# Perceiver block on one core: the last two pipeline steps written as one tail

## What is computed

```python
x = x + fake_quant(layernorm(x)) @ fake_quant(context)        # context: 1024 x 1024 per sequence
h = layernorm(x); qkv = h @ Wqkv                              # 32 query heads of 32, one k and one v head
x = x + softmax(q k^T * scale + alibi, causal) v @ Wo
h = layernorm(x)
routing = softmax(h @ gate_w.T)                               # 8 experts
x = x + (h * (routing @ in_scale)) @ sign(weight).T * (routing @ out_scale) + bias
```

## Time and profile before

| | us |
|---|---|
| median of 3 runs (range) | 446.04 (445.1 to 447.58) |
| the profiled execution | 443.82 |
| its span on the core | 442.0 |
| mean granted TensorE clock | 0.972 |
| PE busy / DVE / ACT / POOL | 372.8 / 308.6 / 258.2 / 96.0 |

### The profile page before, as it was taken

One profiled execution on the slowest core, in us unless ns is written; L12 is line 12 of the kernel. 1 busy time (PEld: TensorE's weight loads), 2 busy tenths in 40 slices (PEclk: granted clock), 3 DMA queues, 4 the chain that ended last, 5 costly groups with the idle time before them and its releaser, 6 DMA issues.

```text
span 442.0 us, 9600 instructions
## 1 busy us (share of the span) xinstructions
PE 372.8 (84%) x3952; PEld 255.0 (58%) x3952; DVE 308.6 (70%) x586; ACT 258.2 (58%) x308; POOL 96.0 (22%) x116
## 2 busy tenths in 40 slices
PE   0444957996999989998999999999999899889565
PEld 0114936953736946694659555965587558745332
DVE  7658579989856278786878688858785965394331
ACT  4777898747778655765666576757575722241010
POOL 5210010003403203140314041403231312031202
PEclk9999997999899999999999999999999999999859
DMA  7999998799399854675477547774681010001001
GB/s 313 385 381 409 408 380 325 258 364 340 139 366 347 297 177 164 249 239 184 159 285 231 190 149 255 267 216 144 213 313 27 0 49 2 3 1 49 0 0 47
DMA packets 30097, 91.97 MB, mean 208 GB/s; under 512 B 8224, under 2 KB 8224, under 8 KB 30048
## 3 DMA queue, kind: packets, MB, share of 16 engines
q1 hardware_dynamic: 27888, 83.40, 53.4%
q10 hardware_dynamic: 2160, 7.87, 4.7%
HBM read 85.50 MB, written 4.19 MB: 203 GB/s over the span
## 4 chain that ended last, share of the span: by engine, by line
PE 62%; DVE 16%; DMA 8%; ACT 5%; issue 5%; SPq 3%; POOL 0%; POOLq 0%; DVEq 0%; ACTq 0%
PE R L1512 10%; DMA ring<-ctx 7%; PE T L1335 7%; PE R L1286 7%; PE R L1287 6%; PE R L1288 6%; PE R L1374 5%; PE R L1377 5%; PE R L1376 5%; PE C L1316 4%; PE T L1468 4%; ACT b L524 3%; SPq L348 2%; DVE Pr L982 2%; DVE Wo L830 1%
## 5 line engine op out<-in xcount | busy, mean ns | idle before, releaser
L524 ACT ACTIVATE b<-ring,quant,qpar 128x2048 uint8<-128x2048 f32 x64 | 132.9, 2090 | 11.3 <-DMA ring<-ctx 8.5
L1374 PE MATMUL R<-T_hi,Wqkv_hi 128*128 128x128 f16 x448 | 78.8, 222 | 0.0
L1376 PE MATMUL R<-T_lo,Wqkv_hi 128*128 128x128 f16 x448 | 78.8, 222 | 0.0
L1377 PE MATMUL R<-T_hi,Wqkv_lo 128*128 128x128 f16 x448 | 78.7, 222 | 0.0
L1512 PE MATMUL R<-sgn,XS_hi 128*128 128x512 fp8e4 x128 | 49.7, 388 | 0.0
L1512 PE MATMUL R<-sgn,XS_lo 128*128 128x512 fp8e4 x128 | 49.5, 387 | 0.0
L1316 PE MATMUL C<-b,aT 128*64 128x512 f16 x256 | 37.8, 423 | 13.2 <-ACT b L524 11.2
L1374 PEld LDWEIGHTS R<-T_hi,Wqkv_hi 128*128 128x128 f16 x448 | 45.1, 101 | 0.4
L316 POOL TENSOR_TENSOR Pr<-Pr,mx 128x512 f32<-128x512 f32 x16 | 16.7, 1042 | 130.2 <-DVE mx L987 130.2
L1376 PEld LDWEIGHTS R<-T_lo,Wqkv_hi 128*128 128x128 f16 x448 | 44.5, 99 | 0.2
L1377 PEld LDWEIGHTS R<-T_hi,Wqkv_lo 128*128 128x128 f16 x448 | 44.5, 99 | 0.0
(11 more groups left out here) (145 smaller groups left out, 879.9 us busy)
## 6 DMA issues: line engine op xcount, KB each, us to landing
ring<-ctx SPq DMA_DIRECT2D x64, 1024.0 KB, 6.3
ring<-L_attn_Wo SPq DMA_DIRECT2D x4, 1024.0 KB, 7.7
ring<-L_ffn_weight SPq DMA_DIRECT2D x4, 1024.0 KB, 5.0
out<-X ACTq DMA_DIRECT2D x8, 512.0 KB, 2.6
Wo<-L_attn_Wqkv SPq DMA_DIRECT2D x7, 544.0 KB, 15.7
X<-x ACTq DMA_DIRECT2D x7, 512.0 KB, 4.0
sgn<-L_attn_Wqkv SPq DMA_DIRECT2D x1, 544.0 KB, 18.4
X<-x SPq DMA_DIRECT2D x1, 512.0 KB, 12.7
```

Of the source, the lines that this page charges most:

```text
L524: e.activation(b8[:, c % BRING, :], ring[:, slot, :], ACT.Identity, scale=qR2, bias=qZ2).then_inc(s_rf[slot], 1)
L1374: e.matmul(dst, hi, rows[0], start=k == 0 and g == 0, stop=False, skip_group_check=True)
L1376: e.matmul(dst, hi, rows[1], start=False, stop=False, skip_group_check=True)
L1377: last = e.matmul(dst, lo, rows[0], start=False, stop=k == KT - 1, skip_group_check=True)
```

## The change

- PE, ACT, DVE and POOL each get a function tail that replaces steps 8 and 9. Steps 0 to 7 are as before.
- Tile 6's sign burst writes C0 and C1 in place of R2 and R3, so pv no longer waits for tile 6's results. Its first half runs as 16 matmuls at the start, ahead of the outscale pair. Its second half is issued in pieces of k: 0-1 after the first pt, 2-3 after the last pv, 4-5 after the projections, 6 after t2, 7 after the router.
- The projections run first half low, ta 1, first half high, second half low, second half high.
- The second norm is written into tok in two halves, each with its own semaphore count; t2's second half waits for the second; the router's k 4 to 7 wait for the second copy.
- The scaled rows of tile 7 are made in three parts of 2, 2 and 4 k (the last one's scales in R3); the output scale pair of tile 7 is ahead of its burst.
- Tile 7's sign burst has three column groups: 512, 256 and 256 columns (R2, C0, C1). It runs k 0-1 of all groups first, then k 2-7 of each. Results follow in three parts; the last sum is on DVE, the other two on POOL.
- SP stores tile 6 (after both sums) and tile 7 in three stores, of 512, 256 and 256 columns. In the kernel before ACT issues one store for each tile.

```diff
@@ SP
-            e.wait_ge(s_out, 16 * TILES)
+            e.wait_ge(s_y, (TILES - 1) * 2)
+            store(TILES - 2, slice(0, H))
+            for n in range(2):
+                e.wait_ge(s_y, (TILES - 1) * 2 + n + 1)
+                store(TILES - 1, last_cols[n])
+            e.wait_ge(s_end, 1)
+            store(TILES - 1, last_cols[2])
+            e.wait_ge(s_out, 16 * (TILES + 2))
@@ POOL
+            def tail(t):
+                subtract_max(e, t, 0, 1)
+                subtract_max(e, t, 1, 1)
+                total(t - 1, 0)
+                inv_std(2, t)
+                with_bias(t)
+                total(t - 1, 1)
+                x_t = X[t % XBUFS]
+                for n in range(2):
+                    cols = last_cols[n]
+                    e.wait_ge(s_fe, t * 2 + n + 1)
+                    e.tensor_tensor(x_t[:, cols], x_t[:, cols], XL[:, cols], ALU.add).then_inc(s_y, 1)
@@ ACT
+                if t == TILES - 1:
+                    e.wait_ge(s_y, t * 2)
+            def tail(s, last):
+                exp(s, 0, 0)
+                outscale_copy(s)
+                pt_hi(s, 0, 0)
+                exp(s, 0, 1)
+                exp(s, 1, 0)
+                pt_hi(s, 0, 1)
+                exp(s, 1, 1)
+                pt_hi(s, 1, 0)
+                pt_hi(s, 1, 1)
+                ta_hi(s, 0)
+                ta_hi(s, 1)
+                t2_copy(s, 0)
+                t2_copy(s, 1)
+                router_exp(s)
+                rt_copy(s)
+                e.wait_ge(s_ffn, (TILES - 1) * 2)
+                for c, rows in enumerate(last_rows):
+                    e.wait_ge(s_xs, (TILES - 1) * 2 + c + 1)
+                    hi_part(XS[0][:, rows, :], ln2T[:, rows, :], 1.0, s_xshi)
+                outscale_copy(last)
@@ DVE
+            def tail(s):
+                t = TILES - 1
+                softmax_rest(t)
+                pt_lo(s, 0, 0)
+                result(s, 0)
+                pt_lo(s, 0, 1)
+                attn_rows(s, 0, 0)
+                pt_lo(s, 1, 0)
+                attn_rows(s, 0, 1)
+                pt_lo(s, 1, 1)
+                attn_rows(s, 1, 0)
+                ta_lo(s, 0)
+                attn_rows(s, 1, 1)
+                ta_lo(s, 1)
+                x2(s, 0)
+                x2(s, 1)
+                last_norm2(t)
+                router_max(s)
+                router_probs(s)
+                result(s, 1)
+                last_xs(0)
+                last_xs(1)
+                last_xs_lo(0)
+                last_xs(2)
+                last_xs_lo(1)
+                last_xs_lo(2)
+                for n in range(3):
+                    last_result(n)
+                x_t, cols = X[t % XBUFS], last_cols[2]
+                e.wait_ge(s_fe, t * 2 + 3)
+                e.wait_ge(s_x2b, TILES)
+                e.tensor_tensor(x_t[:, cols], x_t[:, cols], XL[:, cols], ALU.add).then_inc(s_end, 1)
@@ PE
-                if b == 1 and m > 1:
+                if b == 1 and 1 < m < TILES - 1:
                     e.wait_ge(s_fe, (m - 1) * 2 + h + 1)
...
+            def last_ffn(n, chunks):
+                cols = last_cols[n]
+                if n > 0 and chunks[0] == 0:
+                    e.wait_ge(s_fe, (TILES - 2) * 2 + n)
+                for c in chunks:
+                    e.wait_ge(s_xslo, c + 1)
+                    for k in range(last_rows[c].start, last_rows[c].stop):
+                        for part in range(2):
+                            last = e.matmul(last_sums[n], XS[part][:, k, :], sgn[:, k, cols],
+                                            start=k == 0 and part == 0, stop=k == KT - 1 and part == 1)
+                if k == KT - 1:
+                    last.then_inc(s_ffn, 1)
+
+            def tail(s, last):
+                ffn(s, 0, low)
+                ffn(s, 0, high)
+                outscale(s, 0)
+                outscale(s, 1)
+                pt(s, 0, 0)
+                ffn(s, 1, low[:2])
+                pt(s, 0, 1)
+                pv(s, 0, 0)
+                pt(s, 1, 0)
+                pv(s, 0, 1)
+                pt(s, 1, 1)
+                ta(s, 0)
+                pv(s, 1, 0)
+                pv(s, 1, 1)
+                ffn(s, 1, low[2:])
+                project(s, 0, low)
+                ta(s, 1)
+                project(s, 0, high)
+                project(s, 1, low)
+                project(s, 1, high)
+                ffn(s, 1, high[:2])
+                t2(s)
+                ffn(s, 1, high[2:3])
+                router(s)
+                ffn(s, 1, high[3:])
+                router_t(s)
+                for c in range(3):
+                    last_inscale(s, c)
+                outscale(last, 0)
+                outscale(last, 1)
+                for n in range(3):
+                    last_ffn(n, [0])
+                for n in range(3):
+                    last_ffn(n, [1, 2])
```

More of the change, by code:

```diff
@@ L285, in build @@
         s_y = sem("s_y")
+        s_xslo = sem("s_xslo")
+        s_end = sem("s_end")
         s_free = [sem(f"s_free{k}") for k in range(2)]
@@ L335, in query_to, with ffn_to, last_scales @@
             return C[:, n, :] if i == 1 else R[:, 2 + n, :]
+        def ffn_to(t, n):
+            return C[:, n, :] if t == TILES - 2 else R[:, 2 + n, :]
+        last_sums = (R[:, 2, :], C[:, 0, 0:HALF // 2], C[:, 1, 0:HALF // 2])
+        last_cols = (slice(0, HALF), slice(HALF, 3 * HALF // 2), slice(3 * HALF // 2, H))
+        last_rows = (slice(0, 2), slice(2, 4), slice(4, KT))
+        def last_scales(c):
+            return R[:, 3, :] if c == 2 else T[:, Step(TILES).bank(f"is{c}"), 0:HALF // 2]
         def queries_at(i, n):
@@ L395, in _, with store @@
             run_steps(first_half, lambda s: None)
-            e.wait_ge(s_out, 16 * TILES)
+            def store(t, cols):
+                e.dma_start(out_v[t, :, cols], X[t % XBUFS][:, cols]).then_inc(s_out, 16)
+            e.wait_ge(s_y, (TILES - 1) * 2)
[6 more added lines that the diff above has]
+            e.wait_ge(s_out, 16 * (TILES + 2))
         dq = 1.0 / (C_W * C_LN)
@@ L475, in first_half @@
                     return step_1()
-                if s.i < 3:
+                if s.is_step(TILES):
+                    return tail(TILES - 1)
+                if s.i < 3 or s.i > TILES:
                     return
@@ L743, in step_1 @@
                 conv(3, 1)
+            def tail(s, last):
[19 more added lines that the diff above has]
+                outscale_copy(last)
             def first_half(s):
                 f, m, b = s.front, s.middle, s.back
-                if s.i < 3:
+                if s.is_step(TILES):
+                    return tail(s, Step(TILES + 1))
+                if s.i < 3 or s.i > TILES:
                     return
@@ L765, in second_half @@
                     return step_1(s, Step(2))
+                if s.i >= TILES:
+                    return
                 f, m, b, n = s.front, s.middle, s.back, s.next
@@ L1031, in x2, with last_norm2 @@
                     stats(2, x_m, (1,))
+            def last_norm2(m):
+                e.wait_ge(s_Ta, TILES * 2)
+                e.wait_ge(s_rstd[2], m + 1)
+                for n in range(2):
+                    cols = slice(n * HALF, (n + 1) * HALF)
+                    e.tensor_scalar(tok[:, cols], X[m % XBUFS][:, cols], mv[2][:, 0:1],
+                                    rstd[2][:, 1:2], ALU.subtract, ALU.mult).then_inc(s_xl2, 1)
             def norm2(s):
                 m = s.i - 1
[L1035 to L1038, removed]
+                e.wait_ge(s_T1, s.i * 2 + 2)
                 if s.is_step(2):
@@ L1081, in result, with last_xs, last_xs_lo, last_result @@
                 e.wait_ge(s_ffn, t * 2 + n + 1)
-                e.scalar_tensor_tensor(XL[:, cols], R[:, 2 + n, :], 1.0 / C_XS, XL[:, cols],
+                e.scalar_tensor_tensor(XL[:, cols], ffn_to(t, n), 1.0 / C_XS, XL[:, cols],
+                                       ALU.mult, ALU.mult).then_inc(s_fe, 1)
+            def last_xs(c):
+                e.wait_ge(s_is, (TILES - 1) * 2 + c + 1)
+                rows = ln2T[:, last_rows[c], :].rearrange("p k t -> p (k t)")
+                e.scalar_tensor_tensor(rows, last_scales(c), C_XS, rows, ALU.mult, ALU.mult)                    .then_inc(s_xs, 1)
+            def last_xs_lo(c):
+                e.wait_ge(s_xshi, (TILES - 1) * 2 + c + 1)
+                rows = last_rows[c]
+                lo_part(XS[1][:, rows, :], ln2T[:, rows, :], XS[0][:, rows, :], 1.0, s_xslo)
+            def last_result(n):
+                cols = last_cols[n]
+                e.wait_ge(s_ose, TILES)
+                e.wait_ge(s_ffn, (TILES - 1) * 2 + n + 1)
+                e.scalar_tensor_tensor(XL[:, cols], last_sums[n], 1.0 / C_XS, XL[:, cols],
                                        ALU.mult, ALU.mult).then_inc(s_fe, 1)
@@ L1098, in softmax_rest @@
                 row_max(m, 1, 1)
+            def tail(s):
[30 more added lines that the diff above has]
```

(32 more changed lines are left out.)

5 lines of the change are left out of this document (3 added, 2 removed).

## The result

| | before | after |
|---|---|---|
| median (range, runs) | 446.81 (445.1 to 449.0, 4) | 441.4 (440.7 to 442.98, 4) |
| profiled execution, span | 443.82, 442.0 | 441.02, 439.2 |
| mean granted clock | 0.972 | 0.973 |

The ratio is 0.9896 with a 95% interval of [0.9864, 0.9928]. That is 4.6 us of 446.04, the median that stood in the profile before; a fourth run of the kernel before (449.0) has moved its median since, so the two medians of the table lie 5.4 us apart, which is inside the interval too. The forecast for the median was 442.9, from a difference of -3.1 us; the range held.

What follows compares the result with a forecast made beforehand. PE was taken to bound the kernel up to step 7, then full-clock matmuls to 412.4 us, then dependent operations. Terms +1.5 - 0.75 - 1.5 - 0.35 - 2.0 = -3.1 us, applied to the 446.04 median: 442.9 us, range 441.0 to 446.3.

Steps and rivals of the forecast that it cites:

- A: Tile 7's attention and projections, to the second residual sum: 1.5 us longer, from a 1.6 us PE stall behind ta 1.
- The attention front: Tile 7's attention ahead of the first projection: projections start as before, valued at 0, bounds -0.7 and +1.5 us.
- R2: Rival: exp, copy and transpose chain ahead of the projections grows by 1.5 us; 444.4 us, chance 18%.
- B: Second residual sum to the router's end: 0.75 us shorter, router starting about 4.8 us after the sum's start at 1.2 GHz.
- R1: Rival: PE's clock is kept through the second norm, router 1.90 us in place of 3.57; 441.2 us, chance 14%.
- C: Router's end to tile 7's first burst matmul: 1.5 us shorter (0.9 to 1.7), through smaller first scaled-row operations.
- D: Tile 7's sign burst: 0.35 us shorter, one outscale now being ahead of it; 1.3 us to either side.
- that bound: Tile 7's burst: 256-column matmuls take half of 0.217 us, at worst 0.1 more for some of 32, +1 us.
- E: Last matmul to the end of the span: 2.0 us shorter, 1.1 before the last store's issue and 0.9 in the store.
- R4: Rival: the short last stores save nothing (0.9 us less gain), 256-column matmuls cost 0.5 more; 444.3 us, chance 9%.
- R3: Rival: the clock falls in the attention stretch, projections doubled for 2.6 to 5.2 us; 448.0 us, chance 9%.

Runs made afterwards that it cites:

- b1_order: The kernel before with only first half high moved directly behind ta 1 and second half low after it: 447.74 us, ratio 1.0035.
- a1_order: The changed kernel with the projections in the order of before, second half low right behind ta 1: 439.13 us, ratio 0.9832 to the kernel before.
- a1_again: The same kernel as a1_order, measured once more: 439.95 us, ratio 0.9854 to the kernel before.
- a4_two_parts: The changed kernel with tile 7's scaled rows in two parts of 4 k in place of 2, 2 and 4: 443.18 us, ratio 0.9937.
- a2_one_store: The changed kernel with tile 7 written by one 512 KB store from SP after all three sums: 442.16 us, ratio 0.9923.
- b0_same: The kernel before, unchanged, measured again with a second profile: 446.37 us, ratio 0.9989.

## Why the prediction was right

*A, forecast +1.5.* Right in its parts. The wait behind ta 1 was 2.07 us from start to start for 2.05, and b1_order and a1_order show its price from both sides, +1.65 and -1.66. The attention front, which I valued at 0, gave -0.38: projections start 12.53 us after step 8's start, 12.91 before. R2 (the front longer by 1.5) did not happen. So 0 was the right order of size, and the 0.38 are inside my bounds.

*B, -0.75.* The sum is nearly right, its course was not, and that is luck. With the clock at 1.00 in the transposes and 0.50 in the router, as I assumed, a1_order shows 4.82 and 8.36, my 4.8 and -0.76. In the changed kernel the clock fell before the transposes (router start +5.99) and was back for the router (2.02): 1.2 us lost, 1.5 won. R1 thus came in half: not kept, but won back early. In a1_again it came whole, for the same idle 2.62 us, so its 14% was a chance between executions and not between kernels. Of the rows that I held against it, 62.5 to 66.0 and 107.0 to 110.5 show 0.99 and 0.97: the 0.50 comes only behind them. The two halves of the norm took 1.00 us together, 0.56 to the handover of the first.

*C, -1.5.* Measured -1.44; a4_two_parts gives 0.95 of it back, so about two thirds are the smaller first part. That the rest is the output scale that went ahead is reckoned and not tested: in before's trace it stands 0.54 us ahead of the burst's start (427.05 to 427.59).

*D, -0.35.* Measured -0.11. The time at 1.2 GHz behind the burst's start was 4.0 us in place of the 3.5 I took over from before; that is the difference. 256-column matmuls start 0.11 apart, half of 0.217, so that bound wasn't needed.

*E, -2.0.* Measured -2.01: 1.2 us from last matmul to store, as counted, and 2.2 from there. R4 (no gain from short stores) falls with a2_one_store. The Trainium skill, "DMA: Bandwidth & Descriptors", under "Anatomy of one DMA", has 2.0 us plus the bytes, and gives this for transfers issued from GpSimd, which I should have said; these stores are issued by SP. Here a 128 KB store landed in 1.8, a 512 KB one in 2.6. The measurement decides: 2.3 is too long for them, and the 1.6 to 1.7 behind my -0.9 was 0.1 to 0.2 too short.

*R3* (the clock lost in the attention stretch) was seen in none of the traces of the changed kernel or its variants; the one fall in step 8 was in the kernel before, b0_same, where it cost 1.26 us. My 2.6 to 5.2 count 12 or 24 projections at half speed; the 3.53 us of the earlier trace rows that I took them from hold eight matmuls.

*The size.* -3.1 forecast, -3.38 in the traces, -4.0 and -4.6 in the medians. What lies between the last two is within the intervals. The first trace of before was a lucky one: 443.82, under all four timed runs of that comparison. I saw this and applied the difference to the median, and the range held; but a difference counted from such a trace is more likely too small. Depending on which of the two traces of each kernel are paired, it is 3.2 to 5.9 us, and the forecast counted one pair.

## What to carry to other kernels

In a tail where one dependent operation follows the other, count from the last matmul to the last byte: small last pieces of compute, sum and store were worth 2 us here and could be added alone. The transposes of the attention rows go through two other engines before the matmuls that need them. In a queue in program order, a block of work that does not need the result has to stand right behind; taking that block away cost 1.65 us. And look at the granted clock of the tail before the instruction order: matmuls that nobody reads, in gaps where PE waits anyway, brought more (436.25 for 439.95, ratios 0.976 and 0.9854 on two chips) than the order did.

## What was not expected of the hardware

- A short gap can matter: with 0.72 us still empty ahead of the burst the clock fell, with it filled and two more matmuls behind the router it did not (0.50 and 1.00 in the windows above). That is one trace of each, and the two edits were not taken apart.
- A wait of 1.91 us behind a sparse stretch lost the clock in one execution and kept it in another of the same kernel, and so did one of 2.62 us ahead of the router (a1_order, a1_again). One trace of each kernel says too little about the clock.
- DVE's sum of two SBUF operands took 0.79 us beside a POOL sum and 0.42 alone, while results with one operand in PSUM took 0.42 beside POOL too. The Trainium skill, "VectorE: DVE Perf Modes", under "Two Vector instructions with no wait between them", names a second SBUF read interface that VectorE shares with GpSimd; that fits these numbers, and so does DVE's end 0.28 us behind POOL's, but this is one operation in one trace and no run here isolates it.
